# Mixture-of-experts dispatch: an inverse table built by one-hot matmuls, a gather per expert tile, a scatter back to token order

## The reference, cut to what matters

```python
m = _layernorm(x, ln2_g, ln2_b)
probs = jax.nn.softmax(xt @ Wg, axis=-1)
wts, idx = jax.lax.top_k(probs, K)                  # K = 2 of E = 8
wts = wts / jnp.sum(wts, axis=-1, keepdims=True)
h1 = jax.nn.gelu(jnp.einsum('td,edf->etf', xt, W1) + b1[:, None, :])   # F = 1024
ye = jnp.einsum('etf,efd->etd', h1, W2) + b2[:, None, :]
sel = ye[idx, jnp.arange(T)[:, None], :]
moe_out = jnp.sum(wts[..., None] * sel, axis=1)
return x + moe_out                                   # then x + this, and a last layernorm
```

## Time and profile before

| | us |
|---|---|
| median of 3 runs | 2699.68 (2690.28 to 2710.99) |
| the profiled execution | 2698.63 |
| its span, first to last instruction | 2696.9 |
| PE busy | 2176.6 (81%) |
| DVE busy | 1695.1 (63%) |
| ACT busy | 1353.3 (50%) |
| POOL busy | 912.7 (34%) |

### The profile page before, as it was taken

The page is one execution under the profiler, slowest core; times in us unless marked ns, Lnnn a source line. Parts: engine busy times, 40 slices in busy tenths (PEclk is TensorE's granted clock), DMA queues, the critical chain, the costliest instruction groups (busy, mean ns, idle before and its releaser), DMA issues. The chain is left out here.

```text
span 2696.9 us, 38945 instructions
## 1 busy us (share of the span) xinstructions
PE 2176.6 (81%) x12248; PEld 1150.4 (43%) x12249; DVE 1695.1 (63%) x3527; ACT 1353.3 (50%) x2608; POOL 912.7 (34%) x734
## 2 busy tenths in 40 slices
PE   4589898989998989994688989899860099999950
PEld 2244444544444444442222322232230088888840
DVE  4578887787879687673366565556517055555557
ACT  1266666656565666673156565555634043333321
POOL 4454646363555454334211112211125600000036
PEclk9578897868587787676779888887865599999975
DMA  1211201111111111100722222022007211111136
GB/s 44 65 54 30 65 26 57 32 55 40 51 44 48 46 41 36 33 19 16 214 34 40 33 48 40 25 48 33 10 22 283 98 40 47 47 45 45 44 97 179
DMA packets 149329, 153.20 MB, mean 57 GB/s; under 512 B 23537, under 2 KB 141762, under 8 KB 149186
## 3 DMA queue, kind: packets, MB, share of 16 engines
q1 hardware_dynamic: 142034, 134.11, 18.3%
q0 software_dynamic: 6144, 16.79, 2.1%
q10 hardware_dynamic: 1008, 0.54, 0.1%
HBM read 88.69 MB, written 62.65 MB: 56 GB/s over the span
## 5 line engine op out<-in xcount | busy, mean ns | idle before, releaser
L1190 DVE TENSOR_REDUCE NM<-sP 128x1 f32<-128x512 f32 x512 | 331.9, 684 | 250.6 <-PE sP L1077 249.1
L395 POOL TENSOR_TENSOR YZ<-XL 128x1280 f32<-128x1280 f32 x128 | 297.5, 2324 | 425.4 <-DVE XL L681 396.6
L1009 ACT ACTIVATE PT<-tP 128x512 f32<-128x512 f32 x512 | 284.4, 603 | 273.2 <-PE tP L1089 271.7
L470 ACT ACTIVATE YZ<-YZ,gsc 128x512 f32<-128x512 f32 (+3 forms) x512 | 322.2, 655 | 145.9 <-DVE YZ L657 145.4
L668 DVE CUSTOM_DVE_ANT_0 YZ<-SeP,YZ 128x512 f32<-128x512 f32 (+3 forms) x512 | 243.4, 486 | 212.7 <-PE SeP L535 172.9
L454 ACT ACTIVATE XL<-mP 128x512 f32<-128x512 f32 (+1 forms) x384 | 201.2, 525 | 177.1 <-PE mP L545 176.2
L560 PE MATMUL tPa<-ident,YZ 128*128 128x128 f32 x1280 | 275.5, 340 | 0.3
L1446 ACT ACTIVATE H<-hP,B1T 128x256 f32<-128x256 f32 x312 | 130.8, 471 | 264.4 <-PE hP L1504 263.9
L462 ACT ACTIVATE PTa<-tPa 128x512 f32<-128x512 f32 (+1 forms) x384 | 203.0, 529 | 84.6 <-PE tPa L566 80.5
L534 PE MATMUL SeP<-STG 48*128 48x512 f16 (+3 forms) x512 | 183.4, 358 | 65.7 <-DVE mn L668 64.4
L1420 POOL DMA_INDIRECT X<-results_scratch,idx x64 | 67.5, 1055 | 474.9 <-DMA results_scratch<-X 455.7
(11 more groups left out here) (286 smaller groups left out, 4064.2 us busy)
## 6 DMA issues: line engine op xcount, KB each, us to landing
STG<-planes_a_scratch SPq DMA_DIRECT2D x512, 32.0 KB, 1.8
STW<-in_L_ffn_W SPq DMA_DIRECT2D x16, 1024.0 KB, 9.3
STGb<-planes_scratch SPq DMA_DIRECT2D x96, 128.0 KB, 6.3
rows_scratch<-Zb SPq DMA_DIRECT2D x1, 9984.0 KB, 35.8
X<-rows_scratch SPq DMA_DIRECT2D x39, 256.0 KB, 2.8
results_scratch<-X SPq DMA_DIRECT2D x39, 256.0 KB, 2.2
planes_a_scratch<-HI SPq DMA_DIRECT2D x64, 128.0 KB, 1.7
planes_a_scratch<-LO SPq DMA_DIRECT2D x64, 128.0 KB, 1.8
```

The lines of the kernel that those rows point to most:

```text
L395: pool.tensor_tensor(YZ[:, h % NYZ, :], XL[:, h % NXL, :], XL[:, h % NXL, :], ALU.mult).then_inc(y_ready, 1)
L470: act.activation(w, w, ACT.Square, bias=gsc[:, b % 2, 1, i, hh:hh + 1], scale=gsc[:, b % 2, 0, i, hh:hh + 1]).then_inc(hyp_ready, 1)
L1009: act.activation(PT[:, p % 4, par, kt, :], tP[x % 3][:, :], ACT.Exp).then_inc(exp_done, 1)
L1190: dve.tensor_reduce(NM[:, g % 2, col:col + 1], sP[n % 2][:, :], AX.X, ALU.max, negate=True).then_inc(max_done, 1)
```

## The change

Stage B stores the normalized rows of each sequence in token order (`xm_d`, 512 KB each, eight stores), and no longer clears or writes zeros.

Stage C:

- The routing comes first on DVE; the split of `b2` and `B1T` move behind it.
- POOL makes the low parts of the first 6 weight chunks (`AHEAD`), with a plain subtraction; for these ACT first scales the staged chunk in place (`grow`) and then casts it. DVE makes the other 10.
- DVE splits each position into a block (of 128 rows, 78 of them) and a row within it, and compares them with counting rows: `blkhot` (128 x 64 x 78) and `rowhot` (128 x 64 x 128), bf16 zeros and ones. ACT multiplies `blkhot` by the partition number, POOL by the column number; 64 matmuls of 156 columns sum the products into a table that says for each sorted position which token and which choice stands there. Eleven small DVE instructions turn it into `src` (row of `xm_d`) and `dst` (row of the result scratch `yr_d`; positions without a token get a spare row).
- DVE starts its 10 low parts only behind the table.
- In the expert loop POOL issues two indirect gathers (L1417) and two indirect scatters (L1424) per tile, where SP issued one load and one store. SP loads all residuals into `X` beside it.
- The end: SP loads the results of a sequence in order (two DMAs of 512 KB each), DVE works on four token tiles per step, ACT does the normalization, SP stores 512 KB per sequence.
- Buffers move: `XS`, `YS`, `XT` get space of their own, `Y1` and `Y2` lie over the W1 planes.

```diff
+                        b = at_batch(n, 23, 4)
+                        if b is not None:
+                            sp.wait_ge(xn2, NT * (b + 1))
+                            sp.dma_start(xm_d[NT * b:NT * (b + 1)].rearrange("n p c -> p n c"), X[:, NT * b:NT * (b + 1), :]).then_inc(stored_m, 16)
...
+                    for c in range(AHEAD):
+                        hi, lo = planes(c)
+                        pool.wait_ge(w_hi, c + 1)
+                        pool.tensor_tensor(lo, STW[:, c % STGW, :], hi, ALU.subtract).then_inc(w_lo1, 1)
+                    pool.wait_ge(hot_ready, 1)
+                    pool.wait_ge(cst, 11)
+                    pool.tensor_tensor(blkval[:, :, 1, :], blkhot[:, :, :], coln.unsqueeze(2).broadcast_to([P, COLS, BLOCKS]),
+                                       ALU.mult).then_inc(val_ready, 1)
...
+                    pool.wait_ge(idx_ready, 1)
-                    for n in range(N):
-                        for k in range(2):
-                            pool.indirect_dma_start(out=xs_d.rearrange("s p c -> (s p) c"),
...
+                    pool.wait_ge(stored_m, 16 * B)
+                    pool.wait_ge(w_lo2, CHUNKS - AHEAD)
+                    gather(0)
+                    gather(1)
+                    gather(2)
+                    for j in range(SLOTS):
+                        if j + 3 < SLOTS:
+                            gather(j + 3)
+                        scatter(j)
...
+                    pe.wait_ge(hot_ready, 2)
+                    pe.wait_ge(val_ready, 2)
+                    for c in range(COLS):
+                        mm = pe.matmul(hP[2][:, 0:2 * BLOCKS], rowhot[:, c, :], blkval[:, c, :, :].rearrange("p v j -> p (v j)"),
+                                       start=(c == 0), stop=(c == COLS - 1))
...
+                    for b in range(B):
+                        dve.wait_ge(x2_loaded[b], 16)
+                        dve.wait_ge(y_loaded[b], 32)
+                        tiles = range(NT * b, NT * (b + 1))
+                        for n in tiles:
+                            dve.scalar_tensor_tensor(X[:, n, :], Y1[:, n, :], gate[:, 0, n:n + 1], X[:, n, :], ALU.mult, ALU.add).then_inc(z1, 1)
...
```

More of the change, by code:

```diff
@@ L1396, in _ @@
+                    for b in range(B):
+                        sp.wait_ge(o_ready, NT * (b + 1))
+                        sp.dma_start(out_t[b], X[:, NT * b:NT * (b + 1), :]).then_inc(o_stored, 16)
+                    sp.wait_ge(o_stored, 16 * B)
                 @block.gpsimd
@@ L1638, in _ @@
                     chain(dve.tensor_reduce(count, cmp_s, AX.X, ALU.add))
-                    chain(dve.tensor_scalar(expert[:, :], count, -1.0, None, ALU.add))
-                    dve.sem_inc(idx_ready, 1)
-                    for c in range(CHUNKS):
+                    dve.tensor_scalar(expert[:, :], count, -1.0, None, ALU.add).then_inc(expert_ready, 1)
+                    dve.wait_ge(b2_loaded, 16)
+                    rest = b2f[:, 1, :]
+                    chain(dve.tensor_scalar(b2f[:, 0, :], b2f[:, 0, :], SCALE, None, ALU.mult))
@@ new lines, in _ @@
+                    dve.wait_ge(b1_turned, 1)
+                    dve.tensor_copy(B1T[:, :], mis[:, 0:E * FC]).then_inc(b1_ready, 1)
+                    dve.wait_ge(tab_full, 1)
+                    col, row = hP[2][:, BLOCKS:2 * BLOCKS], hP[2][:, 0:BLOCKS]
+                    where, empty, flat, wrap = [tab[:, n, :] for n in range(4)]
+                    chain(dve.tensor_copy(where, col))
+                    chain(dve.tensor_scalar(empty, where, 0.0, None, ALU.is_equal))
+                    chain(dve.tensor_tensor(empty, empty, spare, ALU.mult))
@@ new lines, in _ @@
+                    chain(dve.scalar_tensor_tensor(flat, where, float(P), row, ALU.mult, ALU.add))
+                    chain(dve.tensor_tensor(flat, flat, empty, ALU.add))
+                    chain(dve.tensor_scalar(flat, flat, -float(P), None, ALU.add))
+                    chain(dve.tensor_copy(dst[:, :], flat))
+                    chain(dve.tensor_scalar(wrap, flat, float(N * P), -float(N * P), ALU.is_ge, ALU.mult))
+                    chain(dve.tensor_tensor(wrap, wrap, flat, ALU.add))
@@ L1673, in _, with pair @@
                     split_h(0, 1, 1, 4)
-                    with dve.Fori(0, LOOPS) as q:
+                    def pair(q, first):
                         for s in range(2):
@@ L1677, in _ @@
                             split_x(s, 2 * q + (s + 3), 8 * q + (4 * s + 12), 10 * q + (5 * s + 12))
-                            result(s, 2 * q + (s + 3), 16 * q + 16)
+                            result(s, 2 * q + (s + 3), None if first else 32 * q)
+                    pair(0, True)
+                    with dve.Fori(1, LOOPS) as q:
+                        pair(q, False)
                     last = 2 * LOOPS
@@ new lines, in _, with invert, offset @@
+                    result(1, last + 4, 32 * LOOPS)
+                    result(0, last + 5, 32 * LOOPS + 32)
+                    def invert(b):
+                        dve.wait_ge(sd3, b + 1)
+                        dve.reciprocal(sd[:, b % 2, 1, :], sd[:, b % 2, 0, :]).then_inc(inv_done, 1)
+                    def offset(b):
+                        dve.wait_ge(inv_done, b + 1)
+                        dve.scalar_tensor_tensor(sd[:, b % 2, 2, :], mv[:, b % 2, :, 0], -1.0, sd[:, b % 2, 1, :],
+                                                 ALU.mult, ALU.mult).then_inc(scale_ready, 1)
@@ L1706 @@
+                    invert(B - 1)
+                    offset(B - 1)
 def kernel(**inputs):
```

346 lines of the change are left out of this document (186 added, 160 removed).

## The result

| | before | after |
|---|---|---|
| median of 4 runs each, us | 2699.16 | 2629.19 |
| lowest and highest, us | 2690.28, 2710.99 | 2612.89, 2639.4 |
| profiled execution, us | 2698.63 | 2612.89 |
| its span, us | 2696.9 | 2611.1 |

The ratio is 0.9733, with a 95% interval of 0.9687 to 0.9779: 70.0 us less at the medians. 2655 had been predicted, with 2630 to 2680 as the range: the median lies 0.8 us under it. The sign was right, the gain was sized too small, at 44 us.

A forecast was written before the change was run, and what follows sets the result against it. Stage C was taken to decide: PE bounds its expert loop, and only the routing and weights ahead and the end behind can gain. 12.2 + 0 + 31.0 + 1 = 44.2 us saved gave 2655 us, range 2630 to 2680.

The forecast's parts named there:

- Where the time goes: Stage C: the change can save ahead of the expert loop and behind it; in the loop it can only lose.
- POOL and DVE exclude each other: Routing: POOL's low parts hold DVE out by a shared port lock, so blkhot starts at 2067.6, not 2040.
- Rival 1: Routing: POOL and DVE hardly hinder each other, blkhot starts at 2040; 22 us less, 2633; chance 0.14.
- The term "head": Stage C ahead of the loop, routing through table and weights: PE starts at 2138.8, 12.2 us earlier.
- The term "end": Behind PE's last matmul: 97.8 us become 66.8, saving 31.0, bounds 22 to 41.
- I take 1.45: End: DVE's time per token tile in us, between 1.29 overlapped and 1.73 with gaps; 46.4 us for 32.
- The loop, 0: Expert loop: four POOL issues per tile cost at most 8 us of 11.34 and stay hidden, so 0.
- Rival 3: Expert loop: POOL's four issues bound it, a tile costs 13.1 us instead of 11.34; 2721; chance 0.05.
- The term "stage B": Stage B: no zeros queued beside the first attention tiles; 1 us saved, from 1 lost to 4 saved.

The follow-up runs named there:

- experiment 1: Changed kernel with AHEAD 0, so POOL makes no low part, ACT grows no chunk and DVE makes all 16 behind the table: 2623.73 us, 0.9728 of before.
- experiment 7: Changed kernel with seven low parts ahead on DVE, none on POOL, XS and YS over the first staging buffer, PE waiting later for weights: 2610.39 us, 0.9696.
- Experiment 3: Changed kernel with each token tile of the end going through its four DVE steps one after the other, not four tiles per step: 2641.38 us.
- experiment 6: Changed kernel with each expert tile's two result scatters issued four times, 10 DMA issues per tile on POOL instead of 4: 2712.06 us.
- experiment 5: Changed kernel with the zero store and the clearing of its tile put back into stage B: stage B 757.2 us, stage C 618.0.
- experiment 9: Kernel before, with the zero store moved from the first to the third sequence of stage B: 2713.29 us.

## Where the prediction was right, and which terms were wrong

The mechanisms of the forecast came as told. What failed are three sizes of its sum: the end (-31.0, measured -41.2), the head (-12.2, measured -19.8) and stage B (-1, measured -4.1); with 1.7 lost in the loop that turns 44.2 into 63.4 us. By these parts alone the time would be about 2636, inside the range. The other 6.6 us, which put the median at 2629 and outside it, are less than stage A varies by from one execution to another.

- **Where the time goes.** Right: head and end gain, the loop doesn't. Head and end are wrong in size, not in mechanism.
- **POOL and DVE exclude each other.** Right, and the largest doubt. DVE instructions of 3.4 to 4.2 us stand in the routing, and experiment 1 took them away together with POOL's work. Rival 1, which gave nearly the measured time (2633), is out: it would have had `blkhot` about 21 us after the stage's start, where it came at 44.1. The time near its 2633 came from other terms, mostly the end, and from stage A. A time near a rival's says nothing for it. The rule of the Trainium skill, SBUF — State Buffer, "SBUF: two separate sides", on the exclusive port pair agrees with these rows. The warning in its box, of DMAs issued from POOL, names DVE's two-port modes; the rows of experiment 7 show it for a DVE instruction with two SBUF inputs (2.29 us) as well.
- **The term "head", -12.2, was -19.8.** From the stage's start PE's first transpose was to be at 120.1 us and came at 112.5. `blkhot` came 4.8 us earlier than predicted (44.1 for 48.9), 3.0 of it because a low part takes POOL 4.1 us and not 4.6, most of the rest because DVE had 4.8 us of routing left behind them and not 6.7; the product took 8.4 behind `rowhot`, not 11.8; the matmuls 6.7, not 8.5, since the clock rose among them (0.66 on the mean, and 4.4 us at full clock over 0.66 is 6.7). The failed step of this term is POOL's price per element, taken from instructions of 512 elements, 2.26 ns each. 2048 elements cost 2.0 ns each and 4992 of bf16 1.7. The two subtractions fit a fixed cost of some 0.2 us and 1.9 ns per element; that the product is cheaper still is its type or its form, which no run separates. The tail of weights was 1.0 us longer and the gathers to PE 1.3 longer, 1.6 against the prediction's own rows, which give 4.4 for the second issue and the landing where its sum has 4.7.
- **The term "end", -31.0, was -41.2.** From PE's last matmul to DVE's first instruction 10.1 us, predicted 10.6; after DVE's last batch as predicted within 1. The 46.4 us for 32 token tiles plus 2.8 were 39.0. The step that failed, the largest of all, is "I take 1.45": the earlier trace rows gave 1.29 for instructions that overlap and 1.73 for ones with gaps, I took the middle, and batches of four run at 1.19, even under the lower end. Experiment 3 shows the other case at 1.57.
- **The loop, 0.** Right, at 1.7 in one pair of profiles and 0.1 in the other. Rival 3's mechanism exists (experiment 6), but an issue costs 1.30 us and not 3.3, as no DVE instruction of the loop is over 0.7 us. Something small is open: in five of the nine profiles of after and of variants with the same loop every second tile takes 11.5 or 11.6 us (loops of 449.8 to 451.8), in the other four and in the three of before none does.
- **The term "stage B", -1, was -4.1**, past the end of the bounds (-4). The wait of PE for the first attention tile, which had spoken for a gain, is still there (9.82 us), so that reason was wrong. Most of the gain is the clock's, at two places (experiment 5), which no row of the prediction had looked at; what moved the clock there stays open.
- **The range** was too narrow at its fast side, because the bounds of its terms were. The values taken lay below the middle of their bounds, and still four measured ones lie past the fast end: POOL's low part (4.1 for 4.6 to 6.2), its product (8.4 for 11.3 to 15.1), DVE's token tile (1.19 for 1.29 to 1.73) and stage B (4.1 for 4).

## What to carry to other kernels

An engine that shares a port with the one on the critical path isn't spare: six subtractions on POOL cost DVE's chain 22 us and saved 16, while seven on DVE, at places where the chain could bear them, made the head 14 us shorter. Four independent tiles per step instead of one tile's chain took 1.19 us per tile instead of 1.57, with the same instructions. Size an engine's long instruction by a fixed cost and a slope from two rows of different length, not by scaling a short one.

## What the runs showed of the hardware that was not expected

- A POOL subtraction of 2048 elements (f32 and f16 in, f16 out) takes 4.1 us, and a bf16 product of 4992 about 8.4; DVE's own product of the same shape takes 5.36, and ACT's 4.46.
- DVE instructions of 256 elements that don't depend on one another start 0.40 us apart, though each shows 0.48; with a wait for the one before 0.52.
- POOL's indirect issue takes 0.95 us beside an idle DVE, 1.0 on the mean of the loop, where no DVE instruction is over 0.7 us, and ends 0.8 to 1.1 us behind the end of a long DVE instruction that it meets.
- A 10 MB store on SP's queue holds the next small store 30.58 us (experiment 9); at its old place in the same stage, where the next store comes 29.8 us behind it, nothing of that kind shows.
- TensorE's clock stood at 0.62 and 0.53 in two stretches of B in both profiles of the kernel before, and at 0.98 to 1.00 in all ten of after and its variants, with the zeros put back too, and in the kernel before with the zeros moved: some 3.6 us in code that the change hardly touches.
